# Attention on one NeuronCore: the copy of each unit's sums out of PSUM moves from ACT to DVE

## The chip, the cores and the metric

The kernel runs on one core of a Trainium2 chip, in one launch. The metric is the device time of that core in microseconds (us). Before the change the median of three runs is 851.26 us (850.18 to 851.35).

The engines, as the profile names them: PE multiplies matrices (PEld is its loading of weights), DVE works on vectors, ACT applies functions element by element, POOL is the third elementwise engine, and SP issues transfers. Each engine takes its instructions in the order in which the program gives them, and waits for others by semaphores.

## The reference

Four sequences of 512 tokens with 512 features go through an attention block and a sparse feed-forward block, each with a residual and a layer norm, all in 32-bit floats:

```python
q = (x @ wq).reshape(bsz, toks, NKV, N_REP, HD)     # 8 groups x 4 heads of 16
k, v = (x @ wk), (x @ wv)                           # 8 groups of 16
scores = einsum('bqgrd,bkgd->bgrqk', q, k) / sqrt(HD)
out = einsum('bgrqk,bkgd->bqgrd', softmax(scores), v)
x = layernorm(x + out.reshape(bsz, toks, 512) @ wo)
inter = x @ c1_w.T @ c2_w.T                         # 1792 columns, 56 blocks of 32
idx = argmax of each block                          # one of 32 rows of w1 and w2t each
x = layernorm(x + relu(x . w1[idx]) @ w2t[idx])
```

## The kernel before

The work has three stages: the projections to q, k and v (to about 90 us), attention (to about 436 us), and the output projection with the feed-forward block (to the end). The change is in attention, in `_attend`.

**Units, key tiles, steps.** Attention goes through 32 units (`NU`): a unit is one sequence and one group of four heads that share keys and values. A unit has four tiles of 128 keys (`TT`, index `kt`), and a step is one unit and one key tile, 128 in all.

**PE in a step** (the loop at L695). It computes transposed scores of the four heads, `scores_t` (L654, into one of three banks `ps_st`), with the step's other matmuls between them: after the first two heads come two score matmuls `scores` (L641) of a later unit, then head 2, then `weigh`, then head 3, then two more `scores`. `weigh` (L657 to L670) multiplies the exponentials of the **step before** with v and adds them up in `ps_pv`, one PSUM bank, over the four key tiles of a unit. In the profile its four matmuls are eight rows of L668. There is only one `ps_pv`: `weigh` of key tile 0 of unit n, which stands in step kt = 1 of unit n, begins a new sum in it and first waits until the sums of unit n - 1 have been copied out (L662, semaphore `stage_ready`). A step of the last three units holds four matmuls of the output projection (L681) in place of the `scores`.

**ACT in a step.** Four exps (L509), one for each head, from `ps_st` to `probs`. The matmul of a head waits until the exp three before it is done, since there are three banks; `weigh` waits for all four exps of its step. Once a unit, ahead of the exp of head 3 in step kt = 0, ACT also runs `take_sums` (L476): it waits for the last `weigh` of the unit before and copies `ps_pv` to one of two buffers `stage` (L480). SP stores that buffer to memory (`store_unit`, L192, in SP's order behind the loads of the unit four further on).

**DVE in a step.** The softmax needs each row's maximum ahead of the exps. DVE takes them three units ahead (`AHEAD`): two instructions `row_max` (L543) a step, each over two tiles of scores in one of two double banks `ps_pair`. The first of a step reads the two `scores` matmuls that PE issues ahead of `weigh`, the second the two that PE issues behind `weigh` and head 3. Once a unit, behind the first `row_max` of kt = 1, DVE transposes the maxima of a unit (`turn_max`, L550). POOL has split these into two parts before (L402, L408), and stores and loads them (L314, L324). Three times in all, behind both maxima of kt = 2, DVE computes reciprocals (L557). The last `row_max` is in unit 28, since units 29 to 31 have no unit three further on.

The order on every engine is that of the code; nothing else plans it.

Of the kernel before, what the change touches and what calls it, by code (L numbers as in the profile page):

```python
# [24 lines left out]
ACT = mybir.ActivationFunctionType  # L25
# [10 lines left out]
TT = S // P  # L36
# [6 lines left out]
DMA = 16  # L43
# [8 lines left out]
NU = NB * NKV  # L52
# [20 lines left out]
def _attend(nc, x, xT, w_qkv, wo, c1, c2, w1, dram, overlays, keep, late):  # L73
# [17 lines left out]
    with ExitStack() as ctx:  # L91
# [19 lines left out]
        stage = [sb(f"stage{j}", [P, S]) for j in range(2)]  # L111
# [5 lines left out]
        ps_pv = ps("ps_pv", [P, S])  # L117
# [11 lines left out]
        st_mm, exp_done, pv_done, stage_ready = sem("st_mm"), sem("exp_done"), sem("pv_done"), sem("stage_ready")  # L129
        stage_out, den_in, inverted = sems("stage_out", 2), sem("den_in"), sem("inverted")  # L130
# [11 lines left out]
        def bank(i):  # L142
            return (*ps_st, ps_pv)[i % 4]
# [308 lines left out]
        @block.scalar  # L452
        def _(act):
            def high_w(o):
                act.wait_ge(w_in[o], DMA)
                nc.scalar.activation(w_h[:, :, columns(o)], w_raw[:, :, columns(o)], ACT.Copy).then_inc(w_high, 1)

            def high_x(b, k):
                act.wait_ge(xt_in[k], DMA * (b + 1))
                if b >= 2 and k == 0:  # L460
                    act.wait_ge(projected, TASKS * (b - 1))
                nc.scalar.activation(x_h[b][:, k], x_raw[:, k], ACT.Copy).then_inc(x_high, 1)

            def take_task(b, o):
                i = TASKS * b + o
                act.wait_ge(projected, i + 1)
                if o == VTASK:
                    if b:
                        act.wait_ge(v_turned, b)
                    nc.scalar.activation(v_rows[:], bank(i)[:], ACT.Copy).then_inc(v_copied, 1)  # L470
                    return
                if b >= 2 and o == 0:
                    act.wait_ge(part_out[b % 2], (REP + 1) * DMA * (b // 2))
                nc.scalar.activation(parts[b % 2][:, o, 0], bank(i)[:], ACT.Copy).then_inc(high_out, 1)

            def take_sums(n):  # L476
                act.wait_ge(pv_done, TT * (n + 1))
                if n >= 2:
                    act.wait_ge(stage_out[n % 2], DMA * (n // 2))
                nc.scalar.activation(stage[n % 2][:], ps_pv[:], ACT.Copy).then_inc(stage_ready, 1)  # L480

            high_w(0)
            for k in range(KT):
                high_x(0, k)
            for o in range(1, 4):
                high_w(o)
            take_task(0, 0)
            high_w(4)
            take_task(0, 1)
            high_w(5)  # L490
            for o in range(2, TASKS):
                take_task(0, o)
                if o - 2 < KT:
                    high_x(1, o - 2)
            for b in range(1, NB):
                for o in range(TASKS):
                    take_task(b, o)
                    if b + 1 < NB and 1 <= o <= KT:
                        high_x(b + 1, o - 1)
            for n in range(NU):  # L500
                for kt in range(TT):
                    for r in range(REP):
                        i = (n * TT + kt) * REP + r
                        if r == 3 and kt == 0 and n:
                            take_sums(n - 1)
                        act.wait_ge(st_mm, i + 1)
                        if r == 0 and n * TT + kt >= 2:
                            act.wait_ge(pv_done, n * TT + kt - 1)
                        nc.scalar.activation(probs[kt % 2][:, r], ps_st[i % 3][:], ACT.Exp,  # L509
                                             scale=float(HD) ** -0.5).then_inc(exp_done, 1)  # L510
            take_sums(NU - 1)

        @block.vector
        def _(dve):
            def low_w(o):
                dve.wait_ge(w_high, o + 1)
                nc.vector.tensor_tensor(w_l[:, :, columns(o)], w_raw[:, :, columns(o)],
                                        w_h[:, :, columns(o)].bitcast(F32), ALU.subtract).then_inc(w_split, 1)

            def low_x(b, k):  # L520
                dve.wait_ge(x_high, KT * b + k + 1)
                nc.vector.tensor_tensor(x_l[b][:, k], x_raw[:, k], x_h[b][:, k].bitcast(F32),
                                        ALU.subtract).then_inc(x_low, 1)

            def low_task(b, o):
                i, m = TASKS * b + o, part(b, o)
                dve.wait_ge(high_out, m + 1)
                if b >= 2 and o == 0:
                    dve.wait_ge(part_out[b % 2], (REP + 1) * DMA * (b // 2))
                nc.vector.tensor_tensor(parts[b % 2][:, o, 1], bank(i)[:], parts[b % 2][:, o, 0].bitcast(F32),  # L530
                                        ALU.subtract).then_inc(low_out, 1)

            def take_v(b):
                dve.wait_ge(v_turned, b + 1)
                nc.vector.tensor_copy(v[b][:, :, :, 0:HD],
                                      bank(TASKS * b + VTASK)[:].rearrange("p (k g d) -> p k g d", k=TT, g=NKV)
                                      ).then_inc(v_ready, 1)

            def row_max(pair):

                dve.wait_ge(max_mm, 2 * (pair + 1))
                at = 2 * pair % RING
                nc.vector.tensor_reduce(neg_max[:, at:at + 2], ps_max[pair % 2][:], AX.X, ALU.max,  # L543
                                        negate=True).then_inc(max_red, 1)

            def turn_max(n):
                dve.wait_ge(max_split, n + 1)
                if n >= 2:
                    dve.wait_ge(max_out[n % 2], DMA * (n // 2))
                nc.vector.transpose(max_rows[n % 2][:], max_parts[:].rearrange("p a h j t -> p (a h j t)").bitcast(F32)  # L550
                                    ).then_inc(max_turned, 1)

            def invert(b):
                dve.wait_ge(den_in, DMA * (b + 1))
                if b:
                    dve.wait_ge(rden_out, DMA * b)
                nc.vector.reciprocal(inv_den[:], den[:]).then_inc(inverted, 1)  # L557

            low_w(0)
            for k in range(KT):  # L560
                low_x(0, k)
            for o in range(1, 4):
                low_w(o)
            low_task(0, 0)
            low_w(4)
            low_task(0, 1)
            low_w(5)
            for j in range(QR):
                for a in range(2):
                    nc.vector.memset(k_[j][64 * a + 32:64 * a + 64].bitcast(F32), 1.0).then_inc(ones_set, 1)  # L570
            for o in range(2, VTASK):
                low_task(0, o)
                low_x(1, o - 2)
            for k in range(VTASK - 2, KT):
                low_x(1, k)
            for b in range(1, NB):
                for o in range(VTASK):
                    low_task(b, o)
                    if o == 0:
                        take_v(b - 1)  # L580
                    if b + 1 < NB and o >= 1:
                        low_x(b + 1, o - 1)
                    for pair in pairs_at(b, o):
                        row_max(pair)
                    for n in range(2):
                        if TASKS * b + o == FIRST_MAXIMA + 4 * (n + 1):
                            turn_max(n)
                for pair in pairs_at(b, VTASK):
                    row_max(pair)
            take_v(NB - 1)  # L590
            for n in range(NU):
                for kt in range(TT):
                    step = n * TT + kt
                    for pair in range(2 * step + AHEAD * TILES // 2, 2 * step + 2 + AHEAD * TILES // 2):
                        if pair < NT // 2:
                            row_max(pair)
                        if n + 2 < NU and kt == 1 and pair % 2 == 0:
                            turn_max(n + 2)
                    b, at = divmod(n - NKV, NKV)
                    if kt == 2 and b >= 0 and at == 1:  # L600
                        invert(b)

        @block.tensor
        def _(pe):
# [674 lines left out]
```

## Time and profile before

| | before |
|---|---|
| median of 3 runs | 851.26 us (850.18 to 851.35) |
| the profiled execution | 850.92 us, span 848.9 us |
| PE busy | 816.0 us, 4084 instructions |
| DVE busy | 622.4 us, 804 instructions |
| ACT busy | 388.4 us, 721 instructions |
| POOL busy | 292.1 us, 388 instructions |
| row maxima on DVE, L543 | 256 of 1219 ns |
| exps on ACT, L509 | 512 of 603 ns |
| mean granted clock of PE | 0.989 |

The span reaches from the first to the last instruction; the execution's time has some 2 us around it. Busy shares are averages over the three stages. A matmul's end is modelled in the profile and matmuls overlap, so a busy PE isn't one at its peak. In a row of the timeline the first number is the start in us from the span's beginning, the second the time until the end of the last of the merged instructions; then come engine, line, operation, and in brackets the idle time of the engine before it and what ended that.

### The profile page before, as it was taken

To read this page: it belongs to the slowest core of one execution; us is meant where nothing else is said; L and a number is where in the kernel's file an instruction comes from. 1 tells how busy PE (TensorE), PEld (TensorE's weight loads), DVE (VectorE), ACT (ScalarE), POOL (GpSimd) and SP (SyncE) were. 2 spreads that over 40 slices of the span, in tenths; PEclk is the share of its full clock that TensorE was granted. 3 is DMA by queue.
4 is the path that set the end of the run, shared out by engine and by line. 5 is a ranking of instruction groups with operands and counts; after the bars stand their busy time and mean duration, and the time that the engine had idled before them with its cause. 6 is when DMAs were issued, how large, how long until landed. Compare 5 with 4: busy or idle time off the path is not lost. (4 is left out here: it accounts for less than half of the span.)

```text
span 848.9 us, 11510 instructions
## 1 busy us (share of the span) xinstructions
PE 816.0 (96%) x4084; PEld 503.6 (59%) x4112; DVE 622.4 (73%) x804; ACT 388.4 (46%) x721; POOL 292.1 (34%) x388
## 2 busy tenths in 40 slices
PE   6999999999999999999989879999999999999995
PEld 5867433333333333333447657777777787777773
DVE  5588899999999999996036887558855795578554
ACT  4321788888888888887731022222112111122220
POOL 2212344654675465225303343342211222112221
PEclk9999999999999999999989989999999999999998
DMA  7783252344544453333225532210400040002001
GB/s 222 252 279 123 78 155 84 106 122 123 156 142 109 124 148 117 88 101 102 76 81 188 196 101 84 77 49 4 147 1 1 0 125 1 1 0 100 1 1 49
DMA packets 48224, 83.05 MB, mean 98 GB/s; under 512 B 9544, under 2 KB 13640, under 8 KB 48040
## 3 DMA queue, kind: packets, MB, share of 16 engines
q1 hardware_dynamic: 40448, 64.45, 24.5%
q0 software_dynamic: 7440, 16.76, 6.7%
q10 hardware_dynamic: 280, 1.11, 0.5%
q8 instruction: 33, 0.54, 0.3%
q14 instruction: 23, 0.19, 0.1%
HBM read 54.18 MB, written 28.05 MB: 97 GB/s over the span
## 5 line engine op out<-in xcount | busy, mean ns | idle before, releaser
L543 DVE TENSOR_REDUCE neg_max<-ps_pair 128x2 f32<-128x1024 f32 x256 | 301.4, 1219 | 30.6 <-PE ps_pair L641 30.6
L509 ACT ACTIVATE probs<-ps_st 128x512 f32<-128x512 f32 x512 | 265.8, 603 | 59.3 <-PE ps_st L654 58.3
L654 PE MATMUL ps_st<-q,k 50*128 50x512 f32 x512 | 185.0, 448 | 2.5 <-ACT probs L509 0.4
L654 PEld LDWEIGHTS ps_st<-q,k 50*128 50x128 f32 x512 | 83.4, 185 | 164.9 <-ACT probs L509 158.9
L892 POOL TENSOR_TENSOR g_l<-picked,g_h 128x512 fp32r<-128x512 f32 x56 | 73.0, 1303 | 250.5 <-ACT g_h L942 250.5
L641 PE MATMUL ps_pair<-k,q 48*128 48x512 f32 x512 | 149.1, 440 | 1.9 <-DVE neg_max L543 1.9
L668 PE MATMUL ps_pv<-probs,v 128*32 128x512 f32 x1024 | 136.4, 605 | 0.0
L935 ACT ACTIVATE picked<-ps_h 128x512 f32<-128x512 f32 x56 | 33.5, 598 | 182.4 <-PE ps_h L1156 182.4
L999 DVE STREAM_TRANSPOSE turned<-ps_prep 128x512 f32<-128x512 f32 x56 | 40.0, 715 | 93.3 <-PE ps_prep L1131 93.3
L1156 PE MATMUL ps_h<-xt_h,w_h 128*128 128x512 f32 x224 | 87.9, 392 | 0.5 <-ACT picked L935 0.5
L1156 PE MATMUL ps_h<-xt_l,w_h 128*128 128x512 f32 x224 | 87.5, 391 | 0.0
L1156 PE MATMUL ps_h<-xt_h,w_l 128*128 128x512 f32 x224 | 87.3, 390 | 0.0
L942 ACT ACTIVATE g_h<-picked 128x512 fp32r<-128x512 f32 x56 | 35.4, 633 | 106.1 <-DVE picked L1019 106.1
L1181 PE MATMUL ps_pair<-w_h,g_h 128*128 128x512 f32 x160 | 72.4, 453 | 1.4 <-POOL g_l L892 1.4
L641 PEld LDWEIGHTS ps_pair<-k,q 48*128 48x128 f32 x512 | 63.8, 184 | 13.4 <-issue 6.7
L1181 PE MATMUL ps_pair<-w_h,g_l 128*128 128x512 f32 x160 | 63.7, 398 | 0.0
L1181 PE MATMUL ps_pair<-w_l,g_h 128*128 128x512 f32 x160 | 63.0, 394 | 0.0
L402 POOL CAST max_parts<-neg_max 128x16 fp32r<-128x16 f32 x32 | 6.6, 206 | 128.3 <-DVE neg_max L543 128.3
L1156 PEld LDWEIGHTS ps_h<-xt_h,w_h 128*128 128x128 f32 x224 | 42.2, 188 | 9.6 <-ACT picked L935 0.5
L1156 PEld LDWEIGHTS ps_h<-xt_l,w_h 128*128 128x128 f32 x224 | 42.2, 189 | 9.2
L1156 PEld LDWEIGHTS ps_h<-xt_h,w_l 128*128 128x128 f32 x224 | 42.1, 188 | 9.2
L1026 DVE TENSOR_TENSOR yf<-ps_pair,yf 128x512 f32<-128x512 f32 x16 | 10.8, 675 | 43.0 <-PEq L91 41.0
(141 smaller groups left out, 1174.6 us busy)
## 6 DMA issues: line engine op xcount, KB each, us to landing
operands<-parts POOLq DMA_DIRECT2D x20, 512.0 KB, 3.7
q<-operands SPq DMA_DIRECT2D x64, 128.0 KB, 2.5
sums<-stage SPq DMA_DIRECT2D x32, 256.0 KB, 3.1
x_raw<-xT SPq DMA_DIRECT2D x16, 256.0 KB, 5.0
k<-operands SPq DMA_DIRECT2D x64, 64.0 KB, 2.3
q<-operands SPq DMA_DIRECT2D x64, 64.0 KB, 2.6
att<-sums SPq DMA_DIRECT2D x16, 256.0 KB
yf<-x SPq DMA_DIRECT2D x4, 1024.0 KB, 5.4
```

Source lines behind the costliest of these rows:

```text
L509: nc.scalar.activation(probs[kt % 2][:, r], ps_st[i % 3][:], ACT.Exp, scale=float(HD) ** -0.5).then_inc(exp_done, 1)
L543: nc.vector.tensor_reduce(neg_max[:, at:at + 2], ps_max[pair % 2][:], AX.X, ALU.max, negate=True).then_inc(max_red, 1)
L641: nc.tensor.matmul(ps_max[tile // 2 % 2][:, a], q[n % QR][64 * a:64 * a + STACK, j, t * P:(t + 1) * P], k_[n % QR][64 * a:64 * a + STACK, ...
L654: nc.tensor.matmul(ps_st[i % 3][:], k_[n % QR][64 * a:64 * a + ROWS, kt * P:(kt + 1) * P], q[n % QR][64 * a:64 * a + ROWS, j, :], start=Tr ...
L668: last = nc.tensor.matmul(ps_pv[32 * r:32 * r + VW], v[b][:, kt, g], probs[kt % 2][:, r], start=(kt == 0), stop=(kt == TT - 1))
L892: nc.gpsimd.tensor_tensor(g_l[m % 2][:], picked[m % 2][:], g_h[m % 2][:].bitcast(F32), ALU.subtract).then_inc(g_ready, 1)
L935: nc.scalar.activation(picked[m % 2][:], ps_h[:], ACT.Relu).then_inc(relu_ready, 1)
L942: nc.scalar.activation(g_h[m % 2][:], picked[m % 2][:], ACT.Copy).then_inc(g_high, 1)
L999: nc.vector.transpose(turned[:].rearrange("p n k -> p (n k)"), bank[:]).then_inc(prep_done, 1)
L1026: nc.vector.tensor_tensor(y[b % 2][:, t], ps_out[t][:], y[b % 2][:, t], ALU.add).then_inc(added, 1)
L1156: last = nc.tensor.matmul(ps_h[:], w[:, k, m * P:(m + 1) * P], xx[b % 2][:, k], start=(k == 0 and n == 0), stop=(k == KT - 1 and n == 2))
L1181: last = nc.tensor.matmul(ps_out[t][:], g[m % 2][:, t * P:(t + 1) * P], w2_tile(*w, m), start=(m == 0 and n == 0), stop=(m == MT - 1 and n ...
```

## The change

ACT's `take_sums` goes, with its call ahead of the exp of head 3 in kt = 0 and the one behind the loop. DVE gets a `take_sums` that waits for the same semaphores and copies the same tile to the same buffer. Its call for unit n - 1 stands in the loop of unit n at kt = 1, behind the first `row_max` of the step and ahead of `turn_max`; the copy of the last unit stands behind the loop.

```diff
@@ block.scalar
-            def take_sums(n):
-                act.wait_ge(pv_done, TT * (n + 1))
-                if n >= 2:
-                    act.wait_ge(stage_out[n % 2], DMA * (n // 2))
-                nc.scalar.activation(stage[n % 2][:], ps_pv[:], ACT.Copy).then_inc(stage_ready, 1)
...
                     for r in range(REP):
                         i = (n * TT + kt) * REP + r
-                        if r == 3 and kt == 0 and n:
-                            take_sums(n - 1)
                         act.wait_ge(st_mm, i + 1)
...
-            take_sums(NU - 1)
@@ block.vector
+            def take_sums(n):
+                dve.wait_ge(pv_done, TT * (n + 1))
+                if n >= 2:
+                    dve.wait_ge(stage_out[n % 2], DMA * (n // 2))
+                nc.vector.tensor_copy(stage[n % 2][:], ps_pv[:]).then_inc(stage_ready, 1)
...
                         if pair < NT // 2:
                             row_max(pair)
+                        if kt == 1 and pair % 2 == 0 and n:
+                            take_sums(n - 1)
                         if n + 2 < NU and kt == 1 and pair % 2 == 0:
                             turn_max(n + 2)
...
+            take_sums(NU - 1)
```

## Rows read from the trace of the kernel before

**Rows 1.** Page, part 1: busy us (share of the span) x instructions.
```profile
PE 816.0 (96%) x4084; PEld 503.6 (59%) x4112; DVE 622.4 (73%) x804; ACT 388.4 (46%) x721; POOL 292.1 (34%) x388
```

**Rows 2.** Timeline of PE, unit 9, key tiles 0 to 2.
```profile
184.49 1.06 PE L668 MATMUL ps_pv<-probs,v 128*32 128x512 f32 x8
185.48 0.49 PE L654 MATMUL ps_st<-q,k 50*128 50x512 f32 x1
185.49 0.73 PE L641 MATMUL ps_pair<-k,q 48*128 48x512 f32 x2
...
186.76 0.50 PE L654 MATMUL ps_st<-q,k 50*128 50x512 f32 x1
187.19 1.06 PE L668 MATMUL ps_pv<-probs,v 128*32 128x512 f32 x8
188.18 0.50 PE L654 MATMUL ps_st<-q,k 50*128 50x512 f32 x1
...
189.37 0.50 PE L654 MATMUL ps_st<-q,k 50*128 50x512 f32 x1
189.80 1.07 PE L668 MATMUL ps_pv<-probs,v 128*32 128x512 f32 x8
```

**Rows 3.** Timeline of ACT, the same stretch.
```profile
185.62 0.60 ACT L480 ACTIVATE stage<-ps_pv 128x512 f32<-128x512 f32 x1
186.12 2.06 ACT L509 ACTIVATE probs<-ps_st 128x512 f32<-128x512 f32 x4
188.72 2.07 ACT L509 ACTIVATE probs<-ps_st 128x512 f32<-128x512 f32 x4 [0.54 <-PE ps_st L654]
```

**Rows 4.** Timeline of DVE, the same stretch.
```profile
186.25 2.36 DVE L543 TENSOR_REDUCE neg_max<-ps_pair 128x2 f32<-128x1024 f32 x2 [0.26 <-PE ps_pair L641]
188.53 0.20 DVE L550 STREAM_TRANSPOSE max_rows<-max_parts 128x32 f32<-128x32 f32 x1
188.96 2.35 DVE L543 TENSOR_REDUCE neg_max<-ps_pair 128x2 f32<-128x1024 f32 x2 [0.23 <-PE ps_pair L641]
```

**Rows 5.** Tile ps_pv: DVE's copy; duration ns min/median/max, first and last start.
```profile
L535 DVE COPY v<-ps_pv x2: 680/680/681, 47.8 to 89.8; 128x512 f32<-128x512 f32 x2
```

**Rows 6.** Timeline behind attention: PE starts after DVE alone.
```profile
438.64 0.69 DVE L1026 TENSOR_TENSOR yf<-ps_pair,yf 128x512 f32<-128x512 f32 x1 [41.02 <-PEq L91]
...
439.39 0.80 PE L1143 MATMUL ps_pair<-wo_h,xt_h 128*128 128x512 f32 x1 [3.92 <-DVE yf L1026]
```

**Rows 7.** Windows, 400 to 430 us: busy (x), PEclk, DMA share, GB/s.
```profile
400.00:430.00 30.00, 30.00 (x153) 11.96 (x145) 0.00 (x0) 21.34 (x41) 9.94 (x11) 1.00 0.24 80
```

**Rows 8.** Timeline of SP in unit 6: a unit's store, the next load.
```profile
156.13 0.60 SPq L194 DMA_DIRECT2D sums<-stage  x1
162.35 0.55 SPq L186 DMA_DIRECT2D k<-operands  x1
```

**Rows 9.** Timeline of DVE and of PE around a reciprocal, unit 9.
```profile
192.71 0.94 DVE L557 RECIPROCAL inv_den<-den 128x128 f32<-128x128 f32 x1
...
194.88 0.50 PE L641 MATMUL ps_pair<-k,q 48*128 48x512 f32 x2 [0.50 <-DVE neg_max L543]
```

**Rows 10.** Timeline of PE behind attention: its other long idle stretches.
```profile
470.86 0.50 PE L1143 MATMUL ps_pair<-wo_h,xt_h 128*128 128x512 f32 x1 [1.76 <-DVE yf L1026]
...
492.61 0.59 PE L1167 MATMUL ps_z<-mask_t,first 128*128 128x512 bf16 x1 [3.26 <-DVE picked L1019]
```

**Rows 11.** Windows: PE, PEld, DVE, ACT, POOL busy (x), PEclk, DMA share, GB/s.
```profile
437.80:444.62 6.82, 5.23 (x12) 4.13 (x13) 5.84 (x9) 0.00 (x0) 0.11 (x1) 0.50 0.55 173
...
470.86:489.30 18.44, 17.70 (x74) 13.76 (x75) 15.76 (x34) 0.60 (x1) 3.41 (x4) 1.00 0.53 185
...
492.42:499.23 6.81, 5.26 (x12) 3.85 (x13) 6.71 (x10) 1.63 (x3) 2.71 (x2) 0.50 0.33 101
```

**Rows 12.** Lines of PE at half clock and at full: busy us, mean ns.
```profile
L1181 PE MATMUL ps_pair<-w_h,g_l 128*128 128x512 f32 x3 | 1.9, 632 | 0.0
...
L1156 PE MATMUL ps_h<-xt_h,w_l 128*128 128x512 f32 x8 | 3.1, 390 | 0.0
```

## The prediction

> **What bounds the kernel now.** The page's busy shares come first: PE 96%, DVE 73% [rows 1]. They average over stages, so the next view is the timeline of one unit in the attention loop, engine by engine, because only there does the copy that moves have a place. The reader is to see three things in it.
>
> First, PE's order and pace [rows 2]. A `weigh` (the eight rows of L668) starts at 184.49, 187.19 and 189.80. The second gap, 2.61 us, is a normal step; the first, 2.70, is the step that holds the copy. A step is one chain. From `weigh` to the fourth score matmul is 188.18 - 187.19 = 0.99. ACT then waits for that matmul and starts its exp 0.54 later (188.72) [rows 3]. The exp ends 0.60 later, and PE issues the third score matmul of the next step at 189.37, 0.65 after the exp began. The next `weigh` follows 0.43 later. 0.99 + 0.54 + 0.65 + 0.43 = 2.61: the loop through PE and ACT sets the pace, and neither engine has room to make up time.
>
> Second, what the copy costs ACT now [rows 3]. It runs 185.62 to 186.22. The exp behind it starts at 186.12; its matmul started at 185.48, so without the copy it would start at 186.02. The copy therefore costs 0.10 us a unit, exactly 2.70 - 2.61. A unit is 2.70 + 3 x 2.61 = 10.53 us.
>
> Third, where DVE stands [rows 4]. Its pair of row maxima 186.25 to 188.61 is the second maximum of key tile 0 and the first of key tile 1; the turn of the maxima (L550), which the program puts right behind that first maximum, starts at 188.53. DVE idles about 0.25 us a step for PE. So DVE is nearly full, but it does not set the pace.
>
> **The change, part by part.** *Removed from ACT:* 32 copies. Their price is the 0.10 us above, so at most 31 x 0.10 = 3 us could come back.
>
> *Added to DVE:* 32 copies of the same tile. DVE's own copy of this tile, the same 128x512 elements, took 0.68 us in the earlier stage [rows 5]. Bounds are a DVE turn, 0.20, and a row maximum over 1024 columns, 1.22 [rows 4]; I take 0.68, the same operation on the same tile.
>
> *Moved:* the place counts for more than the length. `weigh` of key tile 0 of unit n starts a new sum in the only `ps_pv`, and waits for the copy of unit n-1 (`stage_ready`, L662). On PE it stands in step kt = 1, where it starts at 187.19 [rows 2]. The copy of before ended at 186.22, a microsecond earlier. The new copy stands on DVE behind the first maximum of kt = 1, which ends at 188.61. It takes the place of the turn, so it starts at 188.53, ends at 189.21, and PE hears of it about 0.06 later (where PE waited for DVE alone, DVE ended at 439.33 and PE started at 439.39 [rows 6]). So `weigh` starts at 188.53 + 0.68 + 0.06 = 189.27 instead of 187.19: **2.08 us later in each such unit**. What stands before the copy is not shortened by its leaving ACT: the second maximum of tile 0 waits for score matmuls issued at 185.49, right behind the previous `weigh` (184.49) and not behind the exp. Hence the 0.10 us saved on ACT only lengthens PE's wait.
>
> Queued behind the waiting `weigh` on PE are the fourth score matmul of that step and two score matmuls for DVE. ACT waits for the first, DVE for the others. All of them start 2.08 us late, and as the chain of 2.61 us has no slack, nothing is regained in the three steps that follow. DVE does not fall behind further: after the copy and the turn it is free at about 189.4, but its next input comes 188.96 - 187.19 = 1.77 after `weigh` [rows 2, 4], now at 191.04. From there the unit is as before: 4.78 + 3 x 2.61 = 12.61 us.
>
> *How many units.* Copies of units 0 to 27 stand behind a first maximum, in the loop of units 1 to 28. From unit 29 on DVE has no maxima left (from 400 to 430 us it did nothing [rows 7]); there the copy starts when `weigh` ends, as on ACT, and is hidden. So 28 x 2.08 = 58.2 us. The last copy ends the stage: 0.68 instead of 0.60 is +0.08, and up to three times 0.10 may be saved in the last units; I count both as nothing together.
>
> *Other queues.* SP stores a unit's sums at 156.13 and issues its next load at 162.35 [rows 8]. The store would be released some 3 us later, still ahead of that load. On POOL the store of the turned maxima moves with the turn, by less than the unit grows. The reciprocal on DVE (L557, three times) delays the maxima behind it by its 0.94 us, and a unit with it is longer by about 0.5 now; it stands behind the maxima of key tile 2, after DVE has been free since the stall, so its price stays [rows 9].
>
> Sum: 850.92 us for the profiled execution + 58.2 = 909.1. The median of the runs is 0.3 us above that execution, which changes nothing here. With the copy's start uncertain by 0.1 either way the stall is 2.0 to 2.2 us, or 56 to 62 us: 907 to 913.
>
> **The clock.** One more term follows from the stall: PE has nothing to do in it. Its third score matmul ends by the model at 186.76 + 0.50 - 0.10 = 187.16, so PE is idle for 2.1 us, 28 times. In this trace an idle stretch of 1.76 us cost no clock, one of 3.26 and one of 3.92 did [rows 6, 10]; the granted clock was 0.50 for 6.82 us behind each [rows 11]. 2.1 lies between. A straight line from 1.76 (none) to 3.26 (always) gives 0.23, or 6 of 28 stalls: an estimate. Price of one fall: a 512-column matmul took 632 ns at half clock and 390 at full [rows 12], a factor 1.62. Of the 2.61 us of a step 0.60 is the exp and 0.05 its handover; the other 1.96 stretched by 1.62 makes the step 3.83. If a fall lasts one step it costs 1.22 us, if it lasts 6.82 us as here, 6.82 x (1 - 2.61 / 3.83) = 2.17; the middle is 1.7. 6 x 1.7 = 10 us. That gives **919 us**. With 2 to 14 falls at those prices it is 911 to 939.
>
> The Trainium skill, "TensorE: Matmul & The Clock Gate", section "A second HAM failure mode: psum-queue depth-cycling", says that short idle stretches of PE in every iteration can make its clock go down and up again over and over. By that rule the falls come in nearly every stall, the rival (c) below; the 1.76 us stretch without a fall speaks against its full force.
>
> **The rivals.**
> (a) Stall and some falls, as above: 919.
> (b) Stall and no fall: 909, own range 905 to 913. For it: 1.76 us without a fall. Against it: 28 chances at 2.1.
> (c) Stall and a fall in each: 28 x (2.08 + 2.17) = 119 more, 970.
> (d) Part of the stall is regained: ACT could have its first three exps of the step done during the stall, and steps behind it run shorter than 2.61. For it: ACT and DVE do idle [rows 3, 4]. Against it: the chain is `weigh` to fourth score to exp to `weigh`, and all of it comes after the stall. If half came back: 880.
> (e) The other side: DVE's idle time absorbs the copy. Four times 0.25 us a unit is 1.0, the copy is 0.68, and ACT gives back 0.10 a unit: 850.92 - 3.1 = 848. It decides if DVE reached the first maximum of kt = 1 before PE reaches `weigh`, that is, if it stood 2.1 us ahead of where rows 4 have it. It cannot run ahead of its input: the maximum before waits for PE [rows 4].
>
> **How the numbers follow.** Chances: (a) 0.50, (b) 0.37, (c) 0.05, (d) 0.05, (e) 0.03. The time is that of (a), 919. The range takes in (a) and (b) with their bounds, 905 to 941, and leaves out (c), (d) and (e). What this kernel's measurement can tell from no change is about 0.2%, 1.7 us. Faster: 0.03, from (e). Within 0.2%: 0.01, what is left of it and of (d). Slower: 0.96.
>
> **What would show it.** Right: `weigh` to `weigh` around the copy is 4.8 us in 28 units and 2.6 in the other steps; DVE's COPY of `stage` takes 0.68 and stands between a maximum and the turn; PE waits for it some 2 us each time, 58 in all; ACT shows no gap for the copy. Stretches of granted clock 0.50 inside the attention loop show (a) or (c), none (b). Wrong: if the first maximum of kt = 1 ends before PE's `weigh` is due, if the steps behind a stall are shorter than 2.61, or if DVE's row before the copy waits for something other than PE. The stage behind the loop, from 439 us on, should keep its length.

## The result, and the profile after

The changed kernel takes 967.9 us (median of four runs, 961.58 to 983.28) against 851.18 us before: a ratio of 1.135, with an interval of 1.125 to 1.145. The ratio leaves out the run of 983.28 us, which is over 2% longer than the shortest. The kernel is slower by about 117 us, twice the 58 us of the stall that the prediction added up. The trace shown here is of that longest run; a second trace of the same kernel, of a run of 964.77 us (e7 below), stands beside it where sizes matter.

The page, parts 1 and 2, answers to [rows 1]. DVE has 21 us more, ACT 16 less; the granted clock, which stood at 9 throughout attention before (a slice is a fortieth of the span, 9 is 90% or more), is at 6 to 8 from slice 5 to slice 21.

```profile
PE 886.8 (90%) x4112; PEld 533.1 (54%) x4112; DVE 643.0 (66%) x836; ACT 372.9 (38%) x689; POOL 292.2 (30%) x388
...
PEclk9999778677787777867779999999999999999998
```

**The stall.** PE's timeline in a unit where the clock stayed full (unit 10) answers to [rows 2]; L668 is `weigh`.

```profile
241.05 1.06 PE L668 MATMUL ps_pv<-probs,v 128*32 128x512 f32 x8
242.04 0.50 PE L654 MATMUL ps_st<-q,k 50*128 50x512 f32 x1
...
243.23 0.49 PE L654 MATMUL ps_st<-q,k 50*128 50x512 f32 x1
245.91 1.07 PE L668 MATMUL ps_pv<-probs,v 128*32 128x512 f32 x8 [2.19 <-DVE stage L548]
246.91 0.50 PE L654 MATMUL ps_st<-q,k 50*128 50x512 f32 x1
...
248.10 0.50 PE L654 MATMUL ps_st<-q,k 50*128 50x512 f32 x1
248.52 1.07 PE L668 MATMUL ps_pv<-probs,v 128*32 128x512 f32 x8
```

From `weigh` to `weigh` around the copy it is 4.86 us (4.78 forecast), and the next step is 2.61 again: nothing is regained. DVE's timeline of the same stretch answers to [rows 4], with line numbers shifted by the change (L534 is `row_max`, L541 the turn, L548 the copy).

```profile
242.82 2.36 DVE L534 TENSOR_REDUCE neg_max<-ps_pair 128x2 f32<-128x1024 f32 x2 [0.34 <-PE ps_pair L641]
245.09 0.68 DVE L548 COPY stage<-ps_pv 128x512 f32<-128x512 f32 x1
245.69 0.20 DVE L541 STREAM_TRANSPOSE max_rows<-max_parts 128x32 f32<-128x32 f32 x1
247.68 2.36 DVE L534 TENSOR_REDUCE neg_max<-ps_pair 128x2 f32<-128x1024 f32 x2 [1.80 <-PE ps_pair L641]
```

The copy takes 0.68 us, starts where the pair of maxima ends, and ends at 245.77; PE starts 0.14 later (0.06 forecast). DVE then waits 1.80 us for PE, so it is not the engine that is short of time. The view of waits, over attention (time in us, how often, the longest), gives the whole:

```profile
DVE neg_max L534 <- PE ps_pair L641: 141.2, 113, 3.2
...
PE ps_pv L668 <- DVE stage L548: 62.2, 28, 2.4
```

PE waits for the copy 28 times, as forecast, and 62.2 us in all (58 forecast). DVE itself waits for PE more than twice as long as that.

**The clock.** Windows from the first `weigh` to the last step that has maxima; columns as in [rows 11], the clock is the third number from the end. First the kernel before, then the trace of 983.28, then that of 964.77 us.

```profile
92.50:396.40 303.90, 300.13 (x1839) 118.54 (x1838) 276.30 (x263) 251.49 (x489) 147.25 (x237) 1.00 0.42 117
```
```profile
94.10:528.70 434.60, 372.20 (x1843) 149.04 (x1842) 293.31 (x291) 237.98 (x462) 147.17 (x237) 0.76 0.28 82
```
```profile
94.60:510.20 415.60, 353.56 (x1843) 139.81 (x1842) 293.21 (x291) 237.83 (x462) 147.42 (x237) 0.82 0.29 86
```

The same work takes 130.7 and 111.7 us more.
```profile
258.04:268.25 10.21, 9.66 (x40) 3.51 (x40) 5.24 (x6) 4.16 (x8) 1.04 (x2) 0.50 0.30 93
```
```profile
258.59 1.94 PE L668 MATMUL ps_pv<-probs,v 128*32 128x512 f32 x8 [2.20 <-DVE stage L548]
...
262.66 1.93 PE L668 MATMUL ps_pv<-probs,v 128*32 128x512 f32 x8
```

The step takes 4.07 us instead of 2.61 (3.83 forecast). Half-clock time lies behind 27 of the 28 stalls in either trace. Behind attention the length stayed: the last copy starts at 567.8 of 981.5 us and 413.7 us follow; before, it starts at 435.5 of 848.9 and 413.4 follow.

### The profile page after: what moved, and what is told of

Its sections match the earlier page's. It is cut to its first block and busy times, and to the rows that moved or that the text cites. A ratio compares the mean times of both kernels' runs of the same rounds, so it can differ in the third digit from the quotient of the medians.

```text
span 981.5 us, 11538 instructions
## 1 busy us (share of the span) xinstructions
PE 886.8 (90%) x4112; PEld 533.1 (54%) x4112; DVE 643.0 (66%) x836; ACT 372.9 (38%) x689; POOL 292.2 (30%) x388
## 5 line engine op out<-in xcount | busy, mean ns | idle before, releaser
L534 DVE TENSOR_REDUCE neg_max<-ps_pair 128x2 f32<-128x1024 f32 x256 | 301.5, 1218 | 145.6 <-PE ps_pair L641 145.4
L668 PE MATMUL ps_pv<-probs,v 128*32 128x512 f32 x1024 | 179.8, 781 | 62.2 <-DVE stage L548 62.2
L654 PE MATMUL ps_st<-q,k 50*128 50x512 f32 x512 | 223.7, 548 | 0.4 <-ACT probs L501 0.4
L654 PEld LDWEIGHTS ps_st<-q,k 50*128 50x128 f32 x512 | 105.1, 231 | 192.3 <-issue 97.6
L641 PE MATMUL ps_pair<-k,q 48*128 48x512 f32 x512 | 191.7, 527 | 1.5 <-DMA q<-operands 1.1
L641 PEld LDWEIGHTS ps_pair<-k,q 48*128 48x128 f32 x512 | 97.4, 237 | 16.3 <-issue 4.2
L668 PEld LDWEIGHTS ps_pv<-probs,v 128*32 128x32 f32 x1024 | 22.9, 119 | 104.0 <-issue 78.3
```

The costliest lines, as they stand in the source:

```text
L641: nc.tensor.matmul(ps_max[tile // 2 % 2][:, a], q[n % QR][64 * a:64 * a + STACK, j, t * P:(t + 1) * P], k_[n % QR][64 * a:64 * a + STACK, ...
L654: nc.tensor.matmul(ps_st[i % 3][:], k_[n % QR][64 * a:64 * a + ROWS, kt * P:(kt + 1) * P], q[n % QR][64 * a:64 * a + ROWS, j, :], start=Tr ...
L668: last = nc.tensor.matmul(ps_pv[32 * r:32 * r + VW], v[b][:, kt, g], probs[kt % 2][:, r], start=(kt == 0), stop=(kt == TT - 1))
```

## The experiments

Two questions: is it the place of the copy or its engine, and is the half clock an effect of the stall? "Loop" is the window from the first `weigh` to the last step that has maxima, 303.9 us at full clock before. Loop, clock and the count of falls are of the traced run; "falls" says how many of the copies of units 0 to 27 have half clock behind them, and `weigh` to `weigh` is that of units at full clock.

| kernel | time, us (median) | `weigh` to `weigh` at the copy | loop, us | clock in it | falls, of 28 |
|---|---|---|---|---|---|
| before | 851.2 | 2.70 | 303.9 | 1.00 | 0 |
| changed | 967.9 | 4.86 | 434.6 / 415.6 | 0.76 / 0.82 | 27 / 27 |
| e1 DVE, behind first maximum of key tile 0 | 847.24 | 2.61 | 301.2 | 1.00 | 0 |
| e3 DVE, behind second maximum of key tile 0 | 893.98 | 3.73 | 347.0 | 0.94 | 8 |
| e4 ACT, in key tile 1 | 964.54 | 4.23 | 402.8 | 0.80 | 21 |
| e2 stall filled, 50 rows, 128 columns | 954.13 | 4.78 | 400.2 | 0.87 | 22 |
| e8 stall filled, 50 rows, 32 columns, 32-bit | 929.68 | 4.77 | 386.3 | 0.91 | 16 |
| e9 stall filled, 128 rows, 128 columns | 909.19 | 4.77 | 362.1 | 1.00 | 0 |
| e5 stall filled, 128 rows, 4 x 32 columns, 32-bit | 909.78 | 4.77 | 362.0 | 1.00 | 0 |
| e6 stall filled, 128 rows, 32 columns, 32-bit | 908.81 | 4.77 | 363.1 | 1.00 | 0 |

**e1: the same copy on DVE, one row maximum further ahead of PE's need.**

```diff
-                        if kt == 1 and pair % 2 == 0 and n:
+                        if kt == 0 and pair % 2 == 0 and n:
                             take_sums(n - 1)
```

> The copy stays on DVE but stands behind the first row maximum of key tile 0 instead of key tile 1. Theory 1 (the place costs, not the engine): the last weigh of a unit ends near 185.55 in the trace of before, the maximum near 186.00, so the copy runs 185.9 to 186.6 and PE's next weigh at 187.19 finds it done; no stall, granted clock 1.00 through attention, a step of 2.61 us throughout, ACT's 0.10 us a unit comes back: 847 to 850 us. Theory 2 (DVE has no room for 0.68 us a unit, whatever the place): about 855 to 870 us, with DVE's maxima later and PE waiting for them.

847.24 us against 851.24: ratio 0.9955, interval 0.9942 to 0.9969. DVE's timeline in unit 9, then PE's `weigh`:

```profile
181.84 2.36 DVE L534 TENSOR_REDUCE neg_max<-ps_pair 128x2 f32<-128x1024 f32 x2 [0.25 <-PE ps_pair L641]
184.11 0.68 DVE L548 COPY stage<-ps_pv 128x512 f32<-128x512 f32 x1
184.71 2.35 DVE L534 TENSOR_REDUCE neg_max<-ps_pair 128x2 f32<-128x1024 f32 x2
186.97 0.20 DVE L541 STREAM_TRANSPOSE max_rows<-max_parts 128x32 f32<-128x32 f32 x1
187.09 2.31 DVE L534 TENSOR_REDUCE neg_max<-ps_pair 128x2 f32<-128x1024 f32 x2
189.64 1.23 DVE L534 TENSOR_REDUCE neg_max<-ps_pair 128x2 f32<-128x1024 f32 x1 [0.24 <-PE ps_pair L641]
```
```profile
182.67 1.06 PE L668 MATMUL ps_pv<-probs,v 128*32 128x512 f32 x8
185.27 1.06 PE L668 MATMUL ps_pv<-probs,v 128*32 128x512 f32 x8
187.88 1.06 PE L668 MATMUL ps_pv<-probs,v 128*32 128x512 f32 x8
```

The copy ends at 184.79, ahead of `weigh` at 185.27. The step that was 2.70 us is 2.60, and DVE's idle 0.25 us a step takes the copy: the two pairs of maxima behind it follow without idle time, and by the third, at 189.64, DVE waits for PE again. So DVE has the room, and ACT's 0.10 us a unit does come back. Rival theory 2 falls. Of the 4.0 us (0.5%), the loop's share is 2.7; attention also began 1.0 us earlier, where nothing was changed. No other version here is faster than the kernel before.

**e3: one maximum later than e1, one earlier than the change.**

```diff
-                        if kt == 1 and pair % 2 == 0 and n:
+                        if kt == 0 and pair % 2 == 1 and n:
                             take_sums(n - 1)
```

> The copy on DVE stands behind the second row maximum of key tile 0, one maximum (1.14 us) earlier than in the changed kernel. Theory 1: copy 187.39 to 188.07 on the clock of the trace of before, handover 0.15, weigh at 188.22 instead of 187.19: a stall of 1.03 us in 28 units, 850.9 + 29 = 880 us if an idle stretch of 1.1 us costs no clock (877 to 884), with weigh to weigh 3.73 around the copy. If any repeated short idle stretch takes the clock, 900 us or more with granted clock 0.50 in many units.

893.98 us, 14 above the forecast. PE in a unit at full clock, then the loop's window:

```profile
208.52 1.06 PE L668 MATMUL ps_pv<-probs,v 128*32 128x512 f32 x8
...
212.26 1.06 PE L668 MATMUL ps_pv<-probs,v 128*32 128x512 f32 x8 [1.05 <-ACT probs L501]
```
```profile
91.50:438.50 347.00, 315.74 (x1843) 125.26 (x1843) 293.05 (x291) 237.88 (x462) 147.38 (x237) 0.94 0.36 103
```

The stall is the forecast one, 3.73 us, though the trace puts PE's wait down to ACT: DVE's copy, 211.43 to 212.11 there, ended last, 0.15 ahead of `weigh`, and ACT's exps were long done. But the clock was not full: 0.94 is 2 x 0.06 x 347 = 42 us at half, and at 0.34 that is the missing 14 us. So an idle stretch of 1.05 us was followed by half clock behind 8 of the 28 stalls here, where the 1.76 us of [rows 10, 11] cost none in the trace of before; e7 below comes back to that stretch.

**e4: the copy on ACT, but late.**

```diff
-                        if r == 3 and kt == 0 and n:
+                        if r == 3 and kt == 1 and n:
                             take_sums(n - 1)
```
(in the kernel before)

> The kernel before, its copy still on ACT, but in front of the exp of head 3 of key tile 1 instead of key tile 0. Theory 1 (place, not engine): the copy starts when the exp of head 2 lets it, near 188.05 on the clock of the trace of before, ends 188.65, weigh near 188.75 instead of 187.19: a stall of 1.5 us in 28 units and up to 1 us in the last three: about 895 us (888 to 902) without falls of the clock; with falls as in the changed kernel up to 945. Rival (ACT is the right engine and the place is nothing): 851 to 854 us.

964.54 us. ACT's copy, on the engine where it was hidden before, now holds PE up; PE's `weigh` and the loop's window are below it.

```profile
246.92 2.06 ACT L509 ACTIVATE probs<-ps_st 128x512 f32<-128x512 f32 x4 [0.73 <-PE ps_st L654]
248.84 0.63 ACT L480 ACTIVATE stage<-ps_pv 128x512 f32<-128x512 f32 x1
```
```profile
245.39 1.07 PE L668 MATMUL ps_pv<-probs,v 128*32 128x512 f32 x8
...
249.62 1.07 PE L668 MATMUL ps_pv<-probs,v 128*32 128x512 f32 x8 [1.56 <-ACT stage L480]
```
```profile
93.30:496.10 402.80, 358.57 (x1843) 144.63 (x1843) 276.51 (x263) 251.66 (x490) 146.91 (x237) 0.80 0.30 89
```

The place decides, not the engine: late on ACT the copy stalls PE as it does late on DVE, and early on DVE it stalls nothing. (That the two late kernels end within 4 us of each other is chance: the stalls are 1.53 and 2.17 us.) The stall itself, 4.23 - 2.70 = 1.53 in 28 units, was forecast well; the upper figure of 945 us was too low. The loop has 98.9 us more: 42.8 of stall and 56 for 161 us at half clock. The last three units, which have a stall of 2.1 us each here (up to 1 forecast), are 15 us longer.

**e2: the stall filled with matmuls.** The bank that they write is overwritten by the next score matmul.

```diff
                 if kt == 0 and n:
+                    i = (n * TT + 1) * REP + 3
+                    pe.wait_ge(exp_done, i - 2)
+                    for _ in range(8):
+                        nc.tensor.matmul(ps_st[i % 3][:], k_[n % QR][64:64 + ROWS, P:2 * P],
+                                         q[n % QR][64:64 + ROWS, 1, :], start=True, stop=True)
                     pe.wait_ge(stage_ready, n)
```

> The changed kernel, with eight extra matmuls of 512 columns on PE in front of the wait for the copy, once in each of 31 units; they write the bank that the next score matmul overwrites, so they add nothing to the output. Theory 1 (the stall is 60.6 us, and the rest of the loss is the clock that falls because PE idles in it): 8 x 0.237 = 1.9 us fill most of the 2.2 us, the granted clock stays 1.00, weigh to weigh stays 4.87 around the copy: 850.9 + 28 x 2.17 = 911.7, so 909 to 916 us. Rival (the clock falls for another reason, or the steps behind a stall are long for another reason): 955 us or more.

954.13 us: the theory as it stood fell. PE around one filled stall (L665 is the filler, L673 `weigh`) and the loop's window:

```profile
243.50 2.09 PE L665 MATMUL ps_st<-q,k 50*128 50x512 f32 x8
245.52 1.83 PE L673 MATMUL ps_pv<-probs,v 128*32 128x512 f32 x8
```
```profile
92.00:492.20 400.20, 396.68 (x2067) 172.00 (x2066) 293.13 (x291) 237.85 (x462) 147.46 (x237) 0.87 0.31 89
```

PE has work from 243.50 on and is 99% busy over the loop by the profile, and still the `weigh` at 245.52 takes 1.83 us instead of 1.06: the clock has fallen. Half clock lies behind 22 of the 28 stalls. The filler also ran in units 29 to 31, where it cost 12 us, which neither forecast had counted; the loop's clock of 0.87 against a forecast 1.00 settles the question without them. "PE idles, so its clock falls" was too simple. What the filler lacks beside `weigh` is rows (50 of 128), or 32-bit passes.

**e5 and e6: the filler in `weigh`'s own form,** in units 1 to 28 alone; e5 with four column groups, e6 with one.

```diff
+                    if n < NU - AHEAD:
...
+                        for _ in range(2):
+                            for r in range(REP):                 # e6: r = 0 alone
+                                nc.tensor.matmul(ps_st[i % 3][32 * r:32 * r + VW], v[b][:, 0, g],
+                                                 probs[0][:, r], start=True, stop=True)
                     pe.wait_ge(stage_ready, n)
```

> The changed kernel, its stall filled in units 1 to 28 by eight extra 32-bit matmuls of weigh's own shape (all 128 rows of the array, four times 32 columns side by side; their output is overwritten). Theory now: what lets the clock fall is not that PE has no matmul, since 50-row matmuls in the stall did not hold it, but that too little of the array works between two weighs. Then these hold it: granted clock 1.00 in nearly all of attention, only the stall is paid, 850.9 + 28 x 2.17 = 912, with a little for the filler 908 to 922 us. Rival (the wait on DVE's semaphore, or the late start of the steps behind it, takes the clock whatever PE does): 945 to 965 us as with the 50-row filler.

> As the kernel with the whole-array filler, but with the first of the four column groups alone: two 32-bit matmuls of 128 rows by 32 columns, about as long in time, a quarter of the array. Theory of the working share of the array: the clock falls nearly as in the changed kernel, 940 to 970 us. Rival (any busy PE with all rows in use holds the clock): 908 to 922 us.

909.78 and 908.81 us. PE around one stall of e5, the filler of e6, then the windows of the loop, e5 and e6:

```profile
242.76 1.92 PE L667 MATMUL ps_st<-probs,v 128*32 128x512 f32 x16
244.78 1.06 PE L675 MATMUL ps_pv<-probs,v 128*32 128x512 f32 x8
```
```profile
243.97 1.88 PE L666 MATMUL ps_st<-probs,v 128*32 128x512 f32 x4
```
```profile
93.10:455.10 362.00, 355.44 (x2291) 131.25 (x2294) 293.05 (x291) 237.87 (x462) 147.45 (x237) 1.00 0.34 99
```
```profile
93.20:456.30 363.10, 355.27 (x1955) 127.78 (x1958) 293.08 (x291) 237.87 (x462) 147.18 (x237) 1.00 0.33 98
```

The clock holds behind every stall, and what is left is the stall: 362.0 - 303.9 = 58.1 us, 28 times 2.07 (e5). With 128 rows, 32 columns hold it as well as four times 32 (my expectation for e6 was wrong).

The trace of e6 shows one fall all the same, at the start of attention, ahead of the first stall:

```profile
90.10:93.20 3.10, 2.89 (x15) 1.44 (x13) 3.10 (x4) 2.53 (x6) 1.45 (x4) 1.00 0.03 5
93.45:96.86 3.41, 3.41 (x16) 1.45 (x8) 1.94 (x3) 1.87 (x5) 0.78 (x1) 0.50 0.08 10
```

From 90.14 to the first `weigh` at 93.22 PE starts nothing but score matmuls of 48 and 50 rows and is busy 2.89 of 3.10 us; half clock follows at 93.45. So the clock can fall without a stall. e3 has the same fall, at 91.7 us; the other nine traces do not.

**e8 and e9: rows or kind of matmul.** e8 is e6 on 50 rows, e9 is e2 on 128 rows (in units 1 to 28).

```diff
 e8: for _ in range(2):
+    nc.tensor.matmul(ps_st[i % 3][0:VW], k_[n % QR][64:64 + ROWS, P:P + VW].bitcast(F32),
+                     q[n % QR][64:64 + ROWS, 1, :].bitcast(F32), start=True, stop=True)
 e9: for _ in range(8):
+    nc.tensor.matmul(ps_st[i % 3][:], k_[n % QR][:, P:2 * P], k_[n % QR][:], start=True, stop=True)
```

> As the kernel with the quarter-array filler (two 32-bit matmuls of 32 columns in the stall of units 1 to 28), but on 50 rows of the array instead of 128. If the rows at work decide: the clock falls in most units, 940 to 965 us, with half-clock time in attention of 80 us or more. If the kind of matmul decides (32-bit, four times as long a column as the 50-row filler that did not hold it): granted clock 1.00 and 906 to 914 us.

> The stall of units 1 to 28 filled with eight matmuls of 512 columns in the replicated 32-bit format of the scores, as in the first filler, but on all 128 rows instead of 50. If the rows at work decide: granted clock 1.00 in attention and 908 to 916 us. If the kind of matmul decides: 940 to 965 us as with the first filler.

929.68 and 909.19 us. The filler and the loop's window, e8 and then e9:

```profile
209.40 1.87 PE L666 MATMUL ps_st<-q,k 50*32 50x512 f32 x4
```
```profile
93.30:479.60 386.30, 379.61 (x1955) 138.37 (x1956) 293.19 (x291) 237.76 (x462) 147.19 (x237) 0.91 0.32 92
```
```profile
204.98 2.05 PE L666 MATMUL ps_st<-k 128*128 128x512 f32 x8
```
```profile
93.60:455.70 362.10, 358.07 (x2067) 157.26 (x2070) 293.07 (x291) 238.04 (x462) 147.76 (x237) 1.00 0.34 99
```

In these runs the rows decide: two pairs that differ in rows go one way each time (e6 holds and e8 falls, e9 holds and e2 falls), in either format. The fillers of a pair also multiply different numbers (e6 exponentials and v, e8 keys and queries), which no run separates from the rows. e8 fell less than forecast (16 stalls of 28, 70 us at half clock, 929.68 us instead of 940 or more), so 50 rows are not nothing; how much of that is the format is open.

**e7: the changed kernel again.**

> The changed kernel once more, unaltered, for a second trace. The stall must be the same 2.17 us in each of 28 units wherever the clock is full; what differs between runs must be the time at half clock inside attention: extra time = 60.6 + about 0.35 us for each us at half clock, so with 150 to 210 us of it 963 to 985 us. If the stall itself differs between runs this falls.

964.77 us; its window stands above. The stall is 4.865 us `weigh` to `weigh`, and 60.6 + 0.35 x 150 = 113 us against 113.5 measured. The two traces differ by 18.5 us in time and by some 60 us in time at half clock, which at 0.34 is 20 us: the spread of the kernel's runs goes with the clock.

The second trace also shows, behind attention, the stretch that [rows 10] has at 470.86 us, of much the same length, and what follows it:

```profile
585.19 0.50 PE L1143 MATMUL ps_pair<-wo_h,xt_h 128*128 128x512 f32 x1 [1.79 <-DVE yf L1026]
...
586.97 0.63 PE L1143 MATMUL ps_pair<-wo_h,xt_h 128*128 128x512 f32 x1
```
```profile
586.34:589.74 3.40, 3.40 (x10) 2.65 (x9) 3.37 (x7) 0.00 (x0) 0.00 (x0) 0.50 0.29 108
```

Here it is followed by half clock. In the eleven traces of this case the stretch is 1.73 to 1.97 us long, and half clock follows in three (e2, e4 and e7).

## Why the prediction was wrong

The direction was right, 919 us was not, and 967.9 lies outside 905 to 941. By its own steps:

- *The loop, and where `weigh` waits:* right (2.70 - 2.61 is 0.09 and not "exactly" 0.10, which changes nothing). e1, e3 and e4 move the copy and the stall follows the place: none, 1.03, 1.53 and 2.17 us.
- *The copy at 0.68 us, behind the first maximum:* right, 0.68.
- *The handover, 0.06:* right where the stall is filled (e5: the copy ends at 244.72, `weigh` starts at 244.78), short in the changed kernel (0.14). Idling alone doesn't make the difference, since the 0.06 was read behind an idle stretch of 3.92 us [rows 6]; what does is open. So the stall was 2.17 instead of 2.08, 60.6 us instead of 58.2.
- *Nothing regained; 28 units; last units and stage behind unchanged:* right. The sum without the clock was 909.1; the three kernels whose clock holds with the stall in place measure 908.8 to 909.8 (their handover is the forecast 0.06).
- *The clock, "6 of 28 stalls" at 1.7 us:* this step failed, the number of falls above all. Half clock came behind 27 of 28, and cost 70 and 51 us in the two traces instead of 10, 2.5 and 1.8 us a stall. The price was nearer, if low: at half clock `weigh` took 1.94 us instead of 1.06, a factor of 1.83 and not 1.62, and a fall lasted 3.41 to 13.65 us where the forecast took a step to 6.82. The straight line from 1.76 us (none) to 3.26 us (always) had two faults. Its lower end was one stretch in one trace: the same stretch is followed by half clock in 3 of 11 traces. And both ends lie between matmuls of 128 rows [rows 10], while in attention PE's matmuls between two `weigh` use 48 or 50. There idle stretches of 1.05, 1.56 and 2.19 us were followed by half clock behind 8, 21 and 27 of 28 stalls (e3, e4, changed); filling the stall with 50-row matmuls left 22 and 16 (e2, e8), with 128-row matmuls none (e5, e6, e9). That a stall among 50-row matmuls costs more than one of equal length among 128-row ones is what 21 of 28 at 1.56 us beside 3 of 11 at 1.73 to 1.97 suggests; no run compares the two at one length.
- *Rival (c), 970 us at 0.05:* it was what happened, in mechanism. That its time is some 2 us from the median is partly luck: its clock term was 61 us, the two traces have 70 and 51. The Trainium skill ("TensorE: Matmul & The Clock Gate", "A second HAM failure mode: psum-queue depth-cycling") says that such falls can come over and over, without a number; the trace agrees, with 27 of 28. I had set the one stretch of 1.76 us against it.

What stays open: why the rows count, and whether the columns do when there are only 50 rows; no run tells, and none was made between 50 and 128 rows.

## What to carry to other kernels

An engine with idle time can take a copy over, but only ahead of the point where the other engines wait for it: look up where the waiting instruction stands in its own engine's order, and put the copy a full step before it. A stall of PE has two prices, its length and what the granted clock does behind it; judge the second by idle stretches among matmuls of the same kind, and when there are none, give it the wide range. One stretch without a fall is one draw: look for it in several traces before a line is drawn through it. If a stall can't be moved, a few matmuls over all rows into a bank that is overwritten anyway can be cheaper than the fall: 909 us instead of 968 here.

## What the runs showed of the hardware

- Matmuls of 50 rows in the stall left 70 to 104 us of the loop at half clock (e8, e2), matmuls of 128 rows none behind a stall, with 32 columns as with 128 (e6, e9).
- The clock also fell behind a stretch in which PE started nothing but 48- and 50-row matmuls: busy 2.89 of 3.10 us, then granted clock 0.50 for 3.41 us (e6, ahead of the first stall).
- The same idle stretch of 1.73 to 1.97 us between 128-row matmuls was followed by half clock in 3 of 11 traces.
- PE shown as 99% busy by the profile (396.68 of 400.20 us, e2) goes with a granted clock of 0.87.
- PE started 0.06 us behind the end of DVE's copy with a filler ahead of it (e5), and 0.14 to 0.15 us behind it in the changed kernel and e3, after 2.19 and 1.05 us of idling; [rows 6] has 0.06 behind 3.92 us of idling.
